# AdaLN block: idle TensorE products in the set-up, biases loaded as rows, fewer table switches, orders written out whole

## What is computed

```python
mod = (silu(c) @ Wmod).reshape(16, 6, 1, 256)           # c: 16x256, Wmod: 256x1536
sa, ca, ga, sb, cb, gb = (mod[:, i] for i in range(6))
ga, gb = (sign(g) * max(|g|, 0.25) for g in (ga, gb))
h = layernorm(x) * (1 + ca) + sa                        # x: 16x512x256
q, k, v = h @ Wq.T + bq, h @ Wk.T + bk, h @ Wv.T + bv
w = softmax(causal(|q @ k.T| / 16))
x = x + ga * ((w @ v) @ Wo.T + bo)
h = layernorm(x) * (1 + cb) + sb
cluster = argmax(calibrate(h @ cluster_sigs.T))         # 8 clusters of 8 experts
tile = argmax(calibrate(h @ sigs.T)) within the cluster
comp = tanh(gelu(h @ W1 + b1) @ W2 + b2)                # 64, then 2 features
mag = relu(comp @ spline_w1[tile] + spline_b1[tile]) @ spline_w2[tile] + spline_b2[tile]
y = layernorm(h + mag * directions[tile] * scale) * gamma + beta
out = x + gb * y
```

## Time and profile before

| | |
|---|---|
| median of 3 runs | 462.34 us |
| profiled execution, whole | 460.97 us |
| its span, first to last instruction | 459.2 us |
| TensorE (PE) busy | 394.8 us, 86% |
| VectorE (DVE) busy | 370.9 us, 81% |
| ScalarE (ACT) busy | 303.8 us, 66% |
| GpSimd (POOL) busy | 58.9 us, 13% |
| DMA, mean rate over the span | 78 GB/s |
| mean granted TensorE clock | 0.951 of full |

### The profile page before, as it was taken

How to read it: one execution, slowest core, us unless ns; L and a number is a source line. 1 busy time by engine, 2 the same in 40 slices (tenths; PEclk the granted TensorE clock), 3 DMA queues, 4 the chain that set the end, 5 groups by cost and what they waited for, 6 DMA issues and landing times. The chain is left out here.

```text
span 459.2 us, 7718 instructions
## 1 busy us (share of the span) xinstructions
PE 394.8 (86%) x2080; PEld 305.9 (67%) x2080; DVE 370.9 (81%) x1383; ACT 303.8 (66%) x660; POOL 58.9 (13%) x97
## 2 busy tenths in 40 slices
PE   3899999999999999999999999999999987716130
PEld 3767867777687778776877687768777865615120
DVE  3387337487749999889988998899889979979996
ACT  2044566875989588857986698759976967645220
POOL 4024203301001011200120021000100100111222
PEclk9999999999999999999999999999999999977555
DMA  8705033003300332623172319220811130306432
GB/s 216 232 8 160 8 114 97 20 10 111 111 1 27 105 101 43 136 75 116 36 127 91 113 25 140 93 91 7 133 47 46 24 47 2 69 21 86 79 66 71
DMA packets 32906, 35.65 MB, mean 78 GB/s; under 512 B 3376, under 2 KB 28448, under 8 KB 32864
## 3 DMA queue, kind: packets, MB, share of 16 engines
q1 hardware_dynamic: 24752, 26.88, 19.3%
q0 software_dynamic: 7536, 7.48, 12.2%
q10 hardware_dynamic: 576, 0.80, 0.5%
HBM read 19.36 MB, written 15.79 MB: 77 GB/s over the span
## 5 line engine op out<-in xcount | busy, mean ns | idle before, releaser
L602 PE MATMUL bank<-v,probsT 128*128 128x257 f32 x320 | 79.0, 382 | 2.9 <-DVE y L2020 1.8
L585 PE MATMUL bank<-h,g 128*128 128x128 f32 (+3 forms) x256 | 78.0, 434 | 1.6 <-DVE negmax L1872 1.0
L575 PE MATMUL bank<-m_ga,h 128*128 128x258 f32 x256 | 65.7, 383 | 1.9 <-DVE y L2020 1.4
L602 PEld LDWEIGHTS bank<-v,probsT 128*128 128x128 f32 x320 | 57.6, 190 | 13.2 <-issue 3.3
L562 PE MATMUL bank<-h,a_sb 128*128 128x512 f32 x128 | 60.2, 593 | 0.0
L575 PEld LDWEIGHTS bank<-m_ga,h 128*128 128x128 f32 x256 | 46.1, 190 | 14.4 <-issue 3.7
L585 PEld LDWEIGHTS bank<-h,g 128*128 128x128 f32 x256 | 42.9, 190 | 18.3 <-issue 9.3
L1130 ACT ACTIVATE g<-bank,g_bias 128x512 f32<-128x512 f32 x32 | 22.0, 687 | 38.2 <-PE bank L562 38.0
L1872 DVE CUSTOM_DVE_ANT_0 probs<-bank,cmask 128x128 f32<-128x128 f32 (+1 forms) x64 | 30.8, 482 | 17.3 <-ACT bank L1137 17.3
L1742 POOL TENSOR_TENSOR m_ga<-m_sb,a_row 128x512 f32<-128x512 f32 x16 | 20.5, 1292 | 182.2 <-DMA a_row<-gate_rows 159.3
L1137 ACT ACTIVATE bank<-bank,v 128x128 f32<-128x128 f32 (+1 forms) x64 | 31.7, 496 | 17.4 <-PE bank L585 14.7
(11 more groups left out here) (178 smaller groups left out, 794.8 us busy)
## 6 DMA issues: line engine op xcount, KB each, us to landing
x<-in_L_attn_x SPq DMA_DIRECT2D x16, 512.0 KB, 3.9
out<-x SPq DMA_DIRECT2D x14, 512.0 KB, 4.8
out<-res POOLq DMA_DIRECT2D x14, 512.0 KB, 6.3
gb_row<-gate_rows SPq DMA_DIRECT2D x16, 256.0 KB, 3.7
a_row<-gate_rows SPq DMA_DIRECT2D x14, 256.0 KB, 3.3
out<-res SPq DMA_DIRECT2D x2, 512.0 KB, 3.3
wide<-in_L_wmod SPq DMA_DIRECT2D x1, 768.0 KB, 13.5
wide<-in_L_wmod ACTq DMA_DIRECT2D x1, 512.0 KB, 5.6
```

The source lines that it names most:

```text
L575: last = mm(ps[:, 0:VW], h[s][:, c, t * P:(t + 1) * P], m_ga[p % 2][s][:, c, :], start=(c == 0), stop=(c == KC - 1))
L585: last = mm(ps[:, 0:w], g[s][:, c, t * P:(t + 1) * P], h[s][:, c, 0:w], start=(c == 0), stop=(c == KC - 1))
L602: last = mm(ps[:, 0:D + 1], probsT[s][t][:, j * P:(j + 1) * P], v_sb[s][:, j, 0:D + 1], start=(j == 0), stop=(j == t))
```

## The change

It has five parts.

- **Idle products.** su_cT issues 8 products of the identity with itself (128 x 128 x 128, float32) between the wait for the identity and the wait for c, and 16 more after the transposes of c. They go to a bank (BUSY_BANK, here bank 0) that su_cT, su_col and su_bT don't use, and nobody reads them.
- **Biases as rows.** bq, bk and bv are loaded as six rows of 128 elements, turned by one transpose on TensorE (su_bT) and copied by VectorE (sd_bT). bo has its own semaphore in_bo, waited for in sd_vb.
- **Table loads.** On ScalarE 2 of the gelu_table and 2 of the exp_table calls are gone: tanh(0), tanh(5) and others stand beside the Gelu of a later group. The order of ScalarE's other steps around them changes too.
- **Orders.** The lists of all engines are new and written out with no loop over k. But for su_bT and sd_bT and the four switches, they hold the same steps.
- **Banks.** BANK gives most steps another bank.

The diff, cut to its core (the new lists have over a thousand lines; of them stand the beginnings on TensorE, ScalarE and VectorE, and the queues):

```diff
-        bq, bk, bv = (sb(n, [P, KC]) for n in ("bq", "bk", "bv"))
+        b_rows = sb("b_rows", [3 * KC, P])
+        b_cols = sb("b_cols", [P, 3 * KC])
+        bq, bk, bv = (b_cols[:, KC * i:KC * (i + 1)] for i in range(3))
...
+        BUSY_BANK = next(b for b in range(8) if b not in (BANK["su_cT"], BANK["su_col"], BANK["su_bT"]))
...
             dma_ga()
-            dma_gb()
             for i in range(0, 2):
                 ldga(1, i)
             ldga(2, 0)
+            dma_gb()
...
+            def busy(bank, n):
+
+                for _ in range(n):
+                    mm(banks[bank][:, 0:P], ident[:, :], ident[:, :], start=True, stop=True)
+
+            def su_bT():
+                pe.wait_ge(in_bias, 48)
+                ps = free("su_bT", (b_rdy, 1))
+                tr(ps[:, 0:3 * KC], b_rows[:, :], ident[0:3 * KC, 0:3 * KC]).then_inc(b_done, 1)
+
             def su_cT():
                 pe.wait_ge(id_ready, 1)
+                busy(BUSY_BANK, 8)
                 pe.wait_ge(in_c, 16)
...
                 last.then_inc(cT_done, 1)
+                busy(BUSY_BANK, 16)
...
-                pe.wait_ge(in_bias, 64)
+                pe.wait_ge(b_rdy, 1)
...
             su_cT()
             su_col()
-            su_bias()
+            su_bT()
             su_gax(0)
             su_A()
+            su_ga()
+            su_wo()
+            su_bias()
+            su_gax(1)
+            for i in range(0, 2):
+                XT(0, 0, i)
+            su_vb()
+            su_M()
+            G_(0, 0, 0)
+            su_colf()
+            G_(0, 0, 1)
+            V_(0, 0, 0)
             su_sig()
...
             ecl(0)
+            for i in range(1, 3):
+                b_abs(1, 1, i)
+            b_pt(1, 0, 3)
+            b_exp(1, 1, 1)
             gelu_table()
...
             c_gs(1)
-            gelu_table()
...
-            tanh(0)
-            exp_table()
...
-            for w, name in ((bq, "bq"), (bk, "bk"), (bv, "bv")):
-                gp.dma_start(w[:, :], col(ins[f"L0_attn_{name}"]), allow_slow_non_contiguous=True).then_inc(in_bias, 16)
-            gp.dma_start(bo_bc[:, :], ins["L0_attn_bo"].rearrange("(o d) -> o d", o=1).broadcast_to([P, D])).then_inc(in_bias, 16)
+            for i, name in enumerate(("bq", "bk", "bv")):
+                gp.dma_start(b_rows[KC * i:KC * (i + 1), :],
+                             ins[f"L0_attn_{name}"].rearrange("(c p) -> c p", p=P)).then_inc(in_bias, 16)
+            gp.dma_start(bo_bc[:, :], ins["L0_attn_bo"].rearrange("(o d) -> o d", o=1).broadcast_to([P, D])).then_inc(in_bo, 16)
...
-            for i in range(0, 2):
-                ms(1, i)
+            ms(1, 0)
             sp_sig()
+            ms(1, 1)
             sp_rest()
...
+            def sd_bT():
+                dve.wait_ge(b_done, 1)
+                v.tensor_copy(b_cols[:, :], banks[BANK["su_bT"]][:, 0:3 * KC]).then_inc(b_rdy, 1)
...
                 dve.wait_ge(vb_done, 1)
+                dve.wait_ge(in_bo, 16)
...
+            sd_st(0)
             sd_silu()
-            sd_st(0)
             sd_nw(0)
             sd_col()
+            sd_bT()
+            sd_gax(0)
             for i in range(2, 4):
                 a_xh(0, 0, i)
-            sd_bias()
-            sd_gax(0)
             sd_st(1)
```

More of the change, by code:

```diff
@@ L705, in _ @@
-            for i in range(0, 2):
+            PT_(0, 0, 2)
+            su_gb()
+            S_(0, 1, 0)
+            V_(0, 1, 2)
+            PT_(0, 0, 3)
+            for i in range(1, 3):
                 S_(0, 1, i)
             AT(0, 0, 2)
-            su_colf()
-            AT(0, 0, 3)
[L710 to L714, removed]
+            PT_(0, 1, 0)
+            XT(1, 0, 0)
+            V_(0, 1, 3)
+            PT_(0, 1, 1)
@@ new lines, in _ @@
+            tanh(1)
+            for i in range(0, 2):
+                a_h(4, 0, i)
+            a_xh(4, 1, 0)
+            b_pt(3, 1, 0)
+            b_abs(3, 1, 2)
+            gelu(2)
+            exp_table()
+            elo(2)
+            b_abs(3, 1, 3)
+            b_exp(3, 1, 1)
+            b_pt(3, 1, 1)
+            for i in range(1, 3):
+                a_xh(4, 1, i)
+            for i in range(2, 4):
+                b_exp(3, 1, i)
+            a_xh(4, 1, 3)
+            for i in range(2, 4):
+                b_pt(3, 1, i)
@@ new lines, in _ @@
+            b_abs(4, 1, 0)
+            c_ga(2, 2)
+            b_abs(4, 1, 1)
+            b_exp(4, 1, 0)
+            c_ga(2, 3)
+            b_pt(4, 0, 2)
+            c_ga(2, 4)
+            for i in range(1, 3):
+                a_xh(5, 0, i)
+            for i in range(5, 7):
+                c_ga(2, i)
+            b_exp(4, 1, 1)
+            gelu_table()
+            tanh(2)
+            a_xh(5, 0, 3)
+            a_xh(5, 1, 0)
+            c_ga(2, 7)
+            b_pt(4, 0, 3)
+            a_h(5, 0, 0)
@@ new lines, in _ @@
+            gelu(3)
+            exp_table()
+            for i in range(2, 4):
+                b_abs(4, 1, i)
+            b_pt(4, 1, 0)
+            a_h(5, 0, 1)
+            elo(3)
+            a_xh(5, 1, 1)
+            b_pt(4, 1, 1)
+            a_xh(5, 1, 2)
+            b_exp(4, 1, 2)
+            b_pt(4, 1, 2)
+            b_exp(4, 1, 3)
+            b_pt(4, 1, 3)
+            a_xh(5, 1, 3)
+            for i in range(0, 2):
+                b_g(5, 0, i)
+            c_gs(4)
+            for i in range(0, 2):
+                a_h(5, 1, i)
@@ new lines, in _ @@
+            y_nw(1, 0)
+            oa(1, 3)
+            y_nw(1, 1)
+            oa(1, 4)
+            a_nw(5, 0)
+            y_nw(1, 2)
+            oa(1, 5)
+            for i in range(0, 2):
+                ob(1, i)
+            a_nw(5, 1)
+            ob(1, 2)
+            oh(2, 1)
+            b_ri(4, 0, 0)
+            b_ttr(4, 0, 3)
+            b_x2(4, 0, 0)
+            ob(1, 3)
+            oa(1, 6)
+            a_nw(5, 2)
+            ob(1, 4)
+            b_v(4, 1, 1)
+            clc(3, 0)
@@ new lines, in _ @@
+            y_nw(2, 2)
+            b_v(5, 1, 1)
+            a_nw(6, 0)
+            oh(3, 1)
+            a_nw(6, 1)
+            b_x2(5, 0, 0)
+            ob(2, 0)
+            oa(2, 2)
+            b_st(5, 0, 0)
+            a_nw(6, 2)
+            oa(2, 3)
+            ob(2, 1)
+            for i in range(4, 6):
+                oa(2, i)
+            ob(2, 2)
+            oa(2, 6)
+            b_ttr(5, 0, 3)
+            a_nw(6, 3)
+            clc(4, 0)
+            ob(2, 3)
+            clc(4, 1)
@@ L2733, in _ @@
+            loc(5, 7)
+            b_v(7, 0, 2)
+            y_st(4, 7)
+            loc(5, 8)
+            y_var(4, 0)
+            loc(5, 9)
+            for i in range(1, 3):
+                y_var(4, i)
+            c_b2(5)
             for i in range(0, 2):
```

2890 lines of the change are left out of this document (1661 added, 1229 removed), and 16 rows, old and new, of the table BANK.

## The result

The changed kernel takes 456.03 us (median of 4 runs, 455.52 to 458.74) against 462.25 of the kernel before beside it (462.14 to 462.89). The ratio is 0.987, with a 95% interval of 0.984 to 0.991: 6.2 us faster. The forecast was 457.0, the range 452.5 to 463.0. The profiled execution has a span of 453.7 us, 5.5 less than the 459.2 of before.

What follows compares the result with a forecast made beforehand. A TensorE-bound stretch, then a VectorE-bound one from 350 us, so the end moves with the main stream's start. Start 4.3 + table loads 1.1 = 5.4 us off; 456.9 on the median, forecast 457.0, range 452.5 to 463.0.

Steps and rivals of the forecast that it cites:

- The start: Set-up: main stream starts earlier by 1.9 (bo's wait) + 4.1 (clock) - 1.4 - 0.3 = 4.3 us, shifting the end.
- 1.4 + 0.3 us given back: Set-up on TensorE: idle products delay gax0 from 10.8 to 12.2 us, 1.4; the added bias transpose costs 0.3.
- Later loads: Set-up: fewer bias elements let later loads land up to 2.0 us earlier; taken as 0, TensorE waiting for none.
- Clock, 4.1 us: Set-up on TensorE: full speed saves 1.0 on gax0, 1.7 on A and 1.4 on 16 one-column products.
- first V sum: Main stream's start: VectorE, busy 9.45 of 10 us from 30 on, may hold this sum by some 1 us.
- Orders written out: Steady stretch, 60 to 350 us: new orders win under 5 us or add a wait per pass; taken as 0.
- Rival 3: TensorE-bound passes loosen: exponentials can't run between two table switches; at 1.3 us per pass, time 466; chance 0.17.
- Table loads: ScalarE: four fewer loads, 5.1 us of work, but it bounds neither stretch; L1220's waits give 0 to 4.6, taken 1.1.
- GpSimd's queue: GpSimd's signature work stands behind ms(1,0), later places shift by a load or two, beside slack; costed at nothing.
- Rival 4: Steady stretch and tail get denser too: 4.3, 4.6 and 1 us, together 10; time 452.4; chance 0.10.
- The pass at 47.0: Sign in the steady stretches: pass length stays 47.0 us; 47.8 or more would show the forecast wrong.
- Rivals 1 and 2: Set-up: idle products delay start or clock stays slow, 460.3 us (0.14); VectorE holds first V sums, 462.3 us (0.09).

Runs made afterwards that it cites:

- b_start: The kernel before with idle products, biases as rows, bo's own semaphore and bias products behind A and Wo; later lists unchanged: 459.19 us, ratio 0.993.
- ap_tables: a_pool with a needless pair of table loads behind each of tanh(1) to tanh(4), eight loads in all: 460.60 us, ratio 0.996.
- ap_tab4: a_pool with a needless pair of table loads behind tanh(2) and tanh(4) only, 23 loads in all: 455.34 us, ratio 0.986.
- a_biascol: The changed kernel with bq, bk and bv loaded element by element as columns, no transpose or copy; bo stays apart: 458.62 us, ratio 0.993.
- a_noidle: The changed kernel without its 24 idle products, all else as it is: 460.58 us, ratio 0.996 to the kernel before.
- a_pool: The changed kernel with GpSimd's list of the kernel before from the products of pair 2 on; other engines' lists untouched: 451.02 us, ratio 0.974.
- a_oneay: The changed kernel with GpSimd's first output sending, ay(0, 0), moved behind three of the four products of pairs 4 and 5: 452.11 us, ratio 0.978.
- b_idle: The kernel before with the same 24 idle products added to su_cT and nothing else: 461.38 us, ratio 0.997.
- a_trans: The changed kernel with each idle product replaced by two transposes of the identity: 457.53 us, ratio 0.989.

## Why the prediction was right, and what in it was wrong

**The start.** The mechanism held: bo apart, clock up before A, stream shifted to its end. The new start alone gave 4.4 us at pair 7 (b_start), the sum had 4.3. Within it, terms were off:

- *Idle products, "1.4 + 0.3 us given back".* The bias transpose was counted twice: the 1.4 is 12.2 - 10.8, and the 12.2 holds it already, so by the forecast's own terms the shift was 4.6. And in after they gave back 0.5: the clock was up at 4.4 us, near the bound of 4.5 and not at the 6.9 worked out from 256-column products in the earlier trace rows (slow from 16.12 to some 21.5 us, where A ends); su_col ended at 10.64 instead of 11.9, and gax0 started at 10.72, where the weights of ga had landed at 1.79 + 8.4 = 10.2. First G 21.53 instead of 23.1. This is not fixed: in ap_tables, with the same first lists, the clock was up at 7.1 us and the first G product came at 22.72. At pair 0 little of that was left (65.2 us against 65.0 in ap_tab4, where it was up at 4.5).
- *Later loads, "I take 0".* Not zero: the weights of ga landed at 10.2 us instead of 10.8, and with single elements (a_biascol) at 11.1. It is worth about half a microsecond.
- *Clock, 4.1 us.* The durations were nearly right (1.86, 1.13, 1.89), but not the reference: without idle products the clock would have risen inside A, since the wide products now come earlier. What the idle products are worth at the first G product, 2.4 us (a_noidle), is the forecast's 4.1 - 1.7 to the digit, from other terms: less won, and less given back.

At pair 0 the new first lists are another 2.5 us ahead (a_pool 65.0 against b_start 67.5), which the forecast put at zero. 1.65 of them stand at the first G product already (21.51 against 23.16): su_sig's 0.45, which the forecast had, and a clock that was up at 4.4 and not at 6.6 us. VectorE, whose 9.45 of 10 us from 30 on in the earlier trace rows made me fear for the first V sum, has 6.32 there now.

**Orders written out, "I take 0".** As far as the runs show, right for the passes. With 23 table loads (ap_tab4) pair 0 to pair 7 takes 392.0 - 65.0 = 327.0 us, as the 399.1 - 72.1 = 327.0 of before. That the two agree to the digit is luck, as each is one execution, but a gain of several us is not there: the later lists of TensorE, ScalarE and VectorE gained little or nothing of their own, if the four loads stand for those that were taken away. The banks, which the forecast costs nowhere, were never changed by themselves. Rival 3 (looser passes) had the right sign for after alone, 330.7, but its mechanism, exponentials caught between switches, was not what made it so.

**Table loads, "bounds neither stretch", 1.1 us.** This step failed. A busy share of 76% (37.87 of 50 us) is no slack: the two experiments put loads into the TensorE-bound stretch, and TensorE stood for them, because xhat, which its next step needs, was queued behind them. A pair cost 0.8 to 2.7 us, and up to 4.3 where the clock fell as well. Four loads came to 3.5 us in the profile and 4.3 in time. That the four loads which the change takes away are worth as much in their own places wasn't tried; that a_pool needs 323.5 us from pair 0 to 7 and ap_tab4 327.0 makes about 3.5 the best estimate, from this pair of kernels. L1220's waits were the wrong place to read it: they say who waits on VectorE, while the one who stood in ap_tab4 was TensorE, for xhat.

**GpSimd's queue, "I cost them at nothing".** This is the largest miss. "Beside slack" failed: the forecast looked at when each product and load would be ready, and not at what an entry held for 68 us has queued behind it, nor at what three products in a row do to VectorE. It cost 5.0 us (after against a_pool), 3.9 of it one entry. The pass to pair 3 is 6.0 us longer (52.2 against 46.2): 3.7 of standing, 1.9 of four G passes at half speed and some tenths until the clock was back.

**The sum.** As measured, in spans: 7.1 up to pair 0 and 3.5 for the passes make 10.6 with the old list of GpSimd, less 0.6 after the last sum: 459.2 - 10.0 = 449.2, a_pool. The new list moves that by 4.5, to 453.7. The forecast had 4.3 + 1.1 + 0 + 0 = 5.4 against 5.5 measured. So 457.0 came within 1 us because terms mis-sized by 2.8 (start and first pass), 2.4 (tables), -4.5 (GpSimd) and -0.6 (after the last sum) cancel. That the number was so near is luck. Rival 4's total of 10 us is what the spans give once GpSimd's list is put back, though from other terms.

**Its signs.** A's passes, 19 loads, the last sum near 394 (394.7) with some 60 us behind it (59.0) and some 49 of 50 us busy (50.00, 49.08, 48.75) came as forecast. "The pass at 47.0" did not: the passes after pair 3 take 46.3 on average, and the one before it 52.2. That is past the 47.8 which the forecast named as its sign of being wrong, though not for rival 3's reason. Rivals 1 and 2 didn't come: A ran at full speed, and no V sum held the stream.

**A version that beats both.** a_pool, 451.02 us, a ratio of 0.974 to before; a_oneay, one moved entry, 452.11.

## What to carry to other kernels

Before costing a reordered queue at nothing, list for each entry that waits long what is queued behind it: what is held comes out as a stack, and a stack collides where single pieces did not (L2187 took 4.36 us here, and 0.20 in a_pool). An engine with a quarter of its time idle can still be on the path of a stretch that another engine bounds, so test it by adding a piece of its work. When you price a stand of TensorE, look at the granted clock behind it: the same stand cost 2.7 us without a fall and 4.3 with one. Warm-up products cost little where the step behind them is done about when the next load lands (10.6 and 10.2 us here), and they hide a slower chain beside them.

## What the runs showed of the hardware

- **GpSimd's products hold VectorE.** Lone products of 1.28 us stretched a VectorE operation to their own length at most (one of L2224 in a_pool took 1.24 us, its median is 0.22). Right behind a sending it was more: up to 2.75 us with one product, 3.93 with two, 4.36 and 4.93 with three. In three of these four the operation began 0.6 to 0.7 us ahead of the first product, while the sending was being issued. All four ended 0.06 to 0.29 us behind the last product (174.06 and 174.00 us in after), so none ended between two products of a stack. A sending with no product behind it left L2187 at 0.20 us (a_pool). What part the sending has in the hold wasn't tested. The operations hit in these four (L2187, L2277, L2333, L1923) read no PSUM bank; the sum into v, which reads one, took its usual 0.42 us beside a product (a_pool, 167.50 us). What makes the difference the traces don't show. A stack does no harm where no such operation is due: in the kernel before three products run one behind the other from 80.21 to 83.95 us, and VectorE has nothing to do beside them until 83.05, when an operation that reads PSUM takes 0.69 us, its usual time (mean 0.68).
- **The granted clock fell during or behind stands of TensorE, and not behind all of them.** In after it was 0.50 from 171.7 us, 1.2 us into the stand of 3.7, until 178.5, 4.3 us after work had begun again. Of two stands of 2.1 us in the same place, one was followed by a fall (ap_tables, 232.4 to 235.8) and one wasn't (ap_tab4); of two pairs of stands of 1.00 and 0.58 us in the last pass, one was (b_idle) and one wasn't (before).
- **Transposes in the place of the idle products brought the clock up** as the products did: by 5.1 us (a_trans), among the 4.4 to 7.5 us at which it was up with the products, and not at 14.8 as with neither (a_noidle).
- **A table load takes its 1.28 us**, with the next instruction at its end (1.28 to 1.30 us from start to start in ap_tables and ap_tab4, the first load apart); what it costs the kernel depends on who waits behind it.
